# One row buffer for three edge passes of a two-layer graph network: gathers issued from the setup on, one a group in the first pass

## What is computed

```python
h = relu(layernorm(x))
# twice: xt = einsum('nd,rde->rne', h, W); msg = xt[rel, src]
#        h = relu(segment_sum(msg, dst) + h @ SW + b)
x = x + h
h = relu(layernorm(x))
edge_input = concat([h[src], h[dst], edge_attr])
msg = layernorm(relu(relu(edge_input @ eW1 + eb1) @ eW2 + eb2)) * eg + ebeta
node_agg = segment_sum(msg, dst)
upd = relu(concat([h, node_agg]) @ nW1 + nb1) @ nW2 + nb2
out = x + layernorm(h + upd) * ng + nbeta
```

## Time and profile before

| | us |
|---|---|
| median of 3 runs (lowest, highest) | 2863.91 (2858.38, 2866.82) |
| the profiled execution's own time | 2855.17 |
| its span, first to last instruction | 2853.5 |
| PE, DVE, ACT, POOL busy | 2187.5, 2023.0, 1541.0, 1821.7 |

### The profile page before, as it was taken

One profiled execution on the slowest core, in us unless ns is written; L12 is line 12 of the kernel. 1 busy time (PEld: TensorE's weight loads), 2 busy tenths in 40 slices (PEclk: granted clock), 3 DMA queues, 4 the chain that ended last, 5 costly groups with the idle time before them and its releaser, 6 DMA issues. The chain is left out here.

```text
span 2853.5 us, 54165 instructions
## 1 busy us (share of the span) xinstructions
PE 2187.5 (77%) x16219; PEld 1892.5 (66%) x16219; DVE 2023.0 (71%) x6854; ACT 1541.0 (54%) x3284; POOL 1821.7 (64%) x1381
## 2 busy tenths in 40 slices
PE   4778999999668899889873665577767766757997
PEld 4668988888668798888872565444444444435765
DVE  6887887878423587676755888676767676755999
ACT  5996656565423354444434877544334333425887
POOL 5763878765667188888866777288777777770000
PEclk9999999999889999999996888888888888888999
DMA  7994555545379644444437999666666666647998
GB/s 237 316 310 130 113 111 102 107 89 102 48 264 362 248 86 88 88 82 88 88 46 242 417 417 414 253 195 194 175 176 190 181 182 179 191 113 294 406 404 344
DMA packets 297971, 576.18 MB, mean 202 GB/s; under 512 B 65872, under 2 KB 147344, under 8 KB 297872
## 3 DMA queue, kind: packets, MB, share of 16 engines
q1 hardware_dynamic: 188112, 485.01, 46.9%
q0 software_dynamic: 109760, 90.00, 19.5%
HBM read 368.35 MB, written 206.50 MB: 201 GB/s over the span
## 5 line engine op out<-in xcount | busy, mean ns | idle before, releaser
L1056 POOL DMA_INDIRECT s<-E_summed,c_scat x392 | 652.1, 1664 | 262.6 <-ACT E_summed L1235 150.0
L1284 PE MATMUL ps<-c_w,E_masked 128*128 128x128 f32 x6272 | 722.6, 276 | 2.2 <-DVE E_masked L1087 2.0
L1284 PEld LDWEIGHTS ps<-c_w,E_masked 128*128 128x128 f32 x6272 | 714.1, 193 | 3.0 <-DVE E_masked L1087 3.0
L1087 DVE SCALAR_TENSOR_TENSOR E_masked<-E_type_row,E_hT 128x512 f32<-128x512 int32 x784 | 484.1, 688 | 74.4 <-ACT E_hT L1204 62.5
L365 POOL DMA_INDIRECT E_src_rows<-s,c_src x392 | 419.8, 1071 | 167.8 <-issue 118.0
L1418 POOL DMA_INDIRECT s<-E_summed,c_scat x196 | 335.8, 1713 | 126.3 <-issue 53.3
L1407 POOL DMA_INDIRECT E_ends<-h,c_near x196 | 220.1, 1123 | 91.0 <-issue 58.8
L1641 PE MATMUL ps<-E_same,E_normal 128*128 128x512 f32 (+3 forms) x392 | 175.1, 610 | 115.6 <-DVE E_normal L1501 115.6
L365 POOL DMA_INDIRECT E_src_rows<-in_x,c_src x196 | 191.6, 978 | 105.7 <-issue 74.3
L1235 ACT COPY E_summed<-ps 128x512 f32<-128x512 f32 x98 | 57.4, 586 | 347.1 <-DMA s<-E_summed,c_scat 347.0
L1641 PEld LDWEIGHTS ps<-E_same,E_normal 128*128 128x128 f32 x392 | 97.2, 259 | 222.5 <-DVE E_normal L1501 122.2
(11 more groups left out here) (134 smaller groups left out, 4378.8 us busy)
## 6 DMA issues: line engine op xcount, KB each, us to landing
s<-N_out SPq DMA_DIRECT2D x147, 512.0 KB, 5.3
N_xin<-in_x SPq DMA_DIRECT2D x98, 512.0 KB, 10.2
N_sin<-s SPq DMA_DIRECT2D x98, 512.0 KB, 6.8
E_dst_row<-in_dst_line SPq DMA_DIRECT2D x147, 256.0 KB, 4.5
E_type_row<-in_type SPq DMA_DIRECT2D x98, 256.0 KB, 3.5
N_xin<-s SPq DMA_DIRECT2D x49, 512.0 KB, 6.3
h<-N_h SPq DMA_DIRECT2D x49, 512.0 KB, 7.8
E_base<-s SPq DMA_DIRECT2D x49, 512.0 KB, 3.6
```

Of the source, the lines that this page charges most:

```text
L1056: pool.indirect_dma_start(s, bass.IndirectOffsetOnAxis(ap=c["scat"][:, k:k + 1], axis=0), summed[:, g % 2, t * D:(t + 1) * D], None, compu ...
L1087: nc.vector.scalar_tensor_tensor(out=masked[:, u % 2, r, :], in0=type_row[:, u, :], scalar=float(r), in1=hT[:, u % 2, :], op0=ALU.is_equal ...
L1284: ins = nc.tensor.matmul(ps[:, 2 + u % 2, t * D:(t + 1) * D], masked[:, u % 2, r, t * P:(t + 1) * P], w[:, r, :], start=(r == 0 and t == 0 ...
```

## The change

One buffer of 49 groups serves all three edge passes. It is allocated before the setup, and the setup issues the first 16 gathers (4 groups, `SETUP_AHEAD`) for E1 once the source indices are there; for this their load has a semaphore of its own, `src_loaded`. N0 goes on to group 40 instead of 36, and E1 then issues one gather a group instead of two. E2 is unchanged (28 groups ahead, two gathers a group). N2 issues all 49 groups for E3, and E3 issues no source gathers; the wrapped slots and the wait for `src_ready` are gone. `w1` and `w2` are released after E2, which makes room for the three groups.

```diff
-N0_AHEAD = 36
+SETUP_AHEAD = 4
+N0_AHEAD = 40
 N1_AHEAD = 28
-N2_AHEAD = 46
+N2_AHEAD = 49
...
-def setup(nc, sb, sem, a):
+def constants(sb):
...
+def setup(nc, sb, sem, c, ps, a, gathers):
...
-    first_loads = [(src[:], a["src"]), (dst[:], a["dst"])]
+    first_loads = [(c["dst"][:], a["dst"]), (c["sl1"][:], a["sl1"])]
...
+            sp.dma_start(src[:], a["src"]).then_inc(src_loaded, 16)
             for out, in_ in first_loads:
                 sp.dma_start(out, in_).then_inc(loaded, 16)
...
             pool.wait_ge(pool_done, 5)
-    return c
+            pool.wait_ge(src_loaded, 16)
+            gathers.issue(pool, a["x"], GT * SETUP_AHEAD)
...
 class Gathers:
-    def __init__(self, sb, sem, name, index, groups=GROUPS_E):
+    def __init__(self, rows, sem, name, index):
...
-                if g >= self.groups:
-                    pool.wait_ge(used, g - self.groups + 1)
...
             for g in range(GROUPS_E):
-                gathers.issue(pool, x, gathers.issued + 2)
+                gathers.issue(pool, x, gathers.issued + (1 if norm else 2))
                 scatter(g)
...
             for g in range(GROUPS_E):
-                sources.issue(pool, a["s2"], sources.issued + 1, src_ready)
                 for q in range(2):
...
+    with ExitStack() as edges:
+        gathered = edges.enter_context(nc.sbuf_tensor("gathered", [P, GROUPS_E * GE], F32))
+        first_rows, second_rows, sources = (
+            Gathers(gathered, sem, name, c["src"]) for name in ("E1_src", "E2_src", "E3_src"))
+        with ExitStack() as relational:
+            for name in ("w1", "w2"):
+                c[name] = relational.enter_context(nc.sbuf_tensor("c_" + name, [P, NREL, D], F32))
+            stage(setup, first_rows)
...
         stage(node_pass_2, sources)
         stage(edge_pass_messages, sources)
```

More of the change, by code:

```diff
@@ L207, in keep @@
         c[name] = sb("c_" + name, shape, dt)
[L208 to L218, removed]
+    for name in ("ident", "sl1", "nb2", "eb2", "sl2", "eW2", "nW2", "eW1s", "eW1d", "nW1x", "nW1m", "b2", "eg",
+                 "ebeta", "ng", "nbeta"):
+        keep(name, [P, D])
@@ new lines, in constants @@
+    keep("eW1e", [DE, D])
+    for name in ("b1", "eb1", "nb1", "eps", "one"):
+        keep(name, [P, 1])
+    keep("earlier", [P, WINDOW * P])
+    for name in ("nb2_parts", "eb2_parts"):
+        keep(name, [3 * QUARTER, 4, D], BF16)
+    keep("parts_weight", [3 * QUARTER, P], BF16)
+    for name in ("src", "dst", "near", "scat"):
+        keep(name, [P, TILES_E], I32)
+    for name in ("dstf", "dump_less_dst", "dump"):
+        keep(name, [P, TILES_E])
+    keep("zeros", [P, D])
+    return c
@@ L219, in setup @@
+def setup(nc, sb, sem, c, ps, a, gathers):
     part = sb("c_part", [P, D], BF16)
     rest = sb("c_rest", [P, D])
[L221 to L227, removed]
-    first_loads = [(src[:], a["src"]), (dst[:], a["dst"])]
[L230 to L233, removed]
+    first_loads = [(c["dst"][:], a["dst"]), (c["sl1"][:], a["sl1"])]
+    for name in ("nb2", "eb2"):
+        first_loads.append((c[name][:], a[name].partition_broadcast(P)))
@@ L243, in setup @@
-    loads.append((keep("nW1x", [P, D])[:], a["nW1"][0:D, :]))
-    loads.append((keep("nW1m", [P, D])[:], a["nW1"][D:2 * D, :]))
+        loads.append((c[name][:], a[name]))
+    loads.append((c["eW1s"][:], a["eW1"][0:D, :]))
+    loads.append((c["eW1d"][:], a["eW1"][D:2 * D, :]))
+    loads.append((c["eW1e"][:], a["eW1"][2 * D:2 * D + DE, :]))
+    loads.append((c["nW1x"][:], a["nW1"][0:D, :]))
+    loads.append((c["nW1m"][:], a["nW1"][D:2 * D, :]))
     for name in ("b2", "eg", "ebeta", "ng", "nbeta"):
-        loads.append((keep(name, [P, D])[:], a[name].partition_broadcast(P)))
+        loads.append((c[name][:], a[name].partition_broadcast(P)))
@@ L247, in setup @@
     for name in ("b1", "eb1", "nb1"):
-        loads.append((keep(name, [P, 1])[:], a[name].unsqueeze(1)))
+        loads.append((c[name][:], a[name].unsqueeze(1)))
+    src_loaded = sem("src_loaded")
+    ident, earlier, eps, one, parts_weight = (c[k] for k in ("ident", "earlier", "eps", "one", "parts_weight"))
+    src, dst, near, dstf, dump_less_dst, dump = (
+        c[k] for k in ("src", "dst", "near", "dstf", "dump_less_dst", "dump"))
+    bias_parts = [c["nb2_parts"], c["eb2_parts"]]
+    zeros = c["zeros"]
@@ L347, with issue @@
 class Gathers:
-    def __init__(self, sb, sem, name, index, groups=GROUPS_E):
+    def __init__(self, rows, sem, name, index):
         self.index = index
-        self.groups = groups
-        self.rows = sb(f"{name}_rows", [P, groups * GE])
+        self.rows = rows
         self.landed = [sem(f"{name}_landed{k}") for k in range(UNROLL)]
         self.issued = 0
-    def issue(self, pool, table, upto, used=None):
+    def issue(self, pool, table, upto):
         while self.issued < min(upto, TILES_E):
-            g, t = divmod(self.issued, GT)
-            if t == 0:
+            g = self.issued // GT
+            if self.issued % GT == 0:
                 wait(pool, self.landed[g % UNROLL], 64 * (g // UNROLL))
-                if g >= self.groups:
-                    pool.wait_ge(used, g - self.groups + 1)
-            at = (g % self.groups * GT + t) * D
             pool.indirect_dma_start(
-                self.rows[:, at:at + D], None, table,
+                self.rows[:, self.issued * D:(self.issued + 1) * D], None, table,
                 bass.IndirectOffsetOnAxis(ap=self.index[:, self.issued:self.issued + 1], axis=0)).then_inc(
@@ L1510, in step @@
                 if n:
-                    h = UNROLL * n[0] + n[1]
-                    wrapped = isinstance(h, int) and h >= sources.groups
-                    source_rows(*n, sources.group(h - sources.groups if wrapped else h))
+                    source_rows(*n, sources.group(UNROLL * n[0] + n[1]))
                     variances(*n)
@@ L1682, in graph_layers @@
     a["xsrc"] = nc.dram_tensor("xsrc", [GROUPS_E * P, GE], F32).ap()
-    c = setup(nc, sb, sem, a)
+    c = constants(sb)
     def stage(build, *args):
@@ L1689, in stage @@
             build(nc, own_sb, sem, c, ps, a, *args)
[L1691 to L1701, removed]
+    with ExitStack() as edges:
[6 more added lines that the diff above has]
+            stage(setup, first_rows)
+            stage(node_product, "N0", a["x"], a["s1"], c["sl1"], True, first_rows)
+            stage(edge_pass_relational, "E1", a["x"], a["s1"], c["w1"], True, first_rows)
+            stage(node_product, "N1", a["s1"], a["s2"], c["sl2"], False, second_rows)
+            stage(edge_pass_relational, "E2", a["s1"], a["s2"], c["w2"], False, second_rows)
         stage(node_pass_2, sources)
```

6 lines of the change are left out of this document (1 added, 5 removed).

## The result

The changed kernel takes **2754.86 us** (median of 4 runs, 2752.66 to 2755.85), the kernel before 2861.14 us in the same comparison (4 runs, 2823.34 to 2866.82): a ratio of 0.967, with an interval of 0.958 to 0.976. The forecast of no change, 2864 us (2848 to 2877), was wrong by 109 us.

What follows compares the result with a forecast made beforehand. Limits differ by block; in E1 and E3 the chain of scatters and their landing. Setup +6.4, E1 -1, N2 +3, E3 -8.3 sum to +0.1 us, 2855 us; shifted to the runs' median 2864 us, range 2848 to 2877.

Steps and rivals of the forecast that it cites:

- Setup: Before N0: 16 gathers delay the first load to 25.9 us; +6.4 us, bounds +3.7 and +10.6; N0 itself 0.
- the saved latency: N0's first load reaches DVE sooner, as the weights are in by then: 1.8 us back, between 0 and 2.7.
- the slower rival: End of setup: stretched gathers hold the barrier, first load at 34.9 us, kernel 11 us slower, 2875 us; chance 0.16.
- N1, E2, N2: N1 and E2 unchanged, 0, wrong if moved over 3 us; N2's twelve more gathers +3 us, bounds 0 and +4.9.
- E1: 36 groups with one gather instead of 26 with two, gathers all but free: -1 us, bounds -4 and 0.
- E3: Ten source gathers fewer on the path, 0.83 us each: -8.3 us, bounds -13 and 0.
- The faster rival: E1 and E3: gathers on POOL's queue are the path, saving 21 and 13 us; kernel -25 us, 2839; chance 0.17.
- the chain: E1: four scatters, their landing, four scatters set the pace, and two gathers fit into the landing; E3 the same with more.

Runs made afterwards that it cites:

- the burst run: Changed kernel, one gather a group in E1 but eight at once ahead of group 12's scatter: 2790.76 us, E1 562.1 us.
- SP's wait: SP's loads held until earlier scatters landed; added in E1 and E3 to the kernel before: 2786.44 us; in E1 to eight gathers at once: 2765.70 us.

## Why the prediction was wrong

**Setup: right.** First load at 26.24 us, forecast 25.9. The 2.4 us from POOL's end to the load came as taken from E3's end, and the saved latency was 2.5 us where I took 1.8. Setup and N0 together: +5.3 us, forecast +6.4. The sixteen gathers took 0.94 to 1.14 us beside DVE's copies, so the slower rival fell. The rule of the Trainium skill's page "SBUF — State Buffer", section "SBUF: two separate sides", by which they would have been stretched, shows no effect here; no row tells which of DVE's copies the rule covers.

**N1, E2, N2: right in size.** N2 +0.8 us (forecast +3). E2 moved by 2.1 us, N1 by 3.8; the latter is over the bound I set, but N1 varies by as much between profiles of the same code.

**E1: the step that failed**, and with it the forecast. I set 11.15 us a group with gathers beside 11.01 without and concluded that the gathers are all but free. Both figures are right; the comparison isn't. I took the 15 groups without gathers for what E1 costs when POOL has nothing else to do. But they came after the gathers in the same run and carried their lag; the burst run has the same 11.0 us after a single push. That the two figures are so close is chance: with two gathers POOL is full (11.06 us even where the loads are kept away from the landing), and without them it waits for a landing that the loads lengthen. The idle time ahead of each scatter, which I read as slack that hides a gather, was this landing, 3.56 us of gap in the mean where the changed kernel has 2.54. The trace held a hint that I cut off: my stretch ended at 714.33, and from 727.47 on the groups take 9.79 us. The forecast was -1 us with bounds of -4 and 0; measured are -50.4 us, by the profiles some 20 of lag and some 30 of POOL filled by two gathers.

**E3: the same step again.** I priced ten gathers at 15.85 - 15.02 = 0.83 us each, -8.3 us. With SP's wait, the kernel before still loses 9 us to the changed one (714.0 against 704.7), so that price was about right for what it measured. The other 52 us are, by that profile, the lag in the groups I had taken as the reference.

**The faster rival** had the direction and not the cause. It gave E1 21 us and E3 13, one gather's 1.32 us for each gather saved; measured are 112 us for 28 gathers, three times that. Its evidence against (11.15 beside 11.01) was the same false comparison. One row did speak: in the earlier trace rows no engine of E1 is busy for more than 86.5% of it. Groups of 11.0 us with no engine full need a reason; I named "the chain" and did not ask why its landing took up to 3.2 us, nor what else was under way meanwhile.

**Left open.** Whether the landing is late because packets of the two queues share the DMA engines or for another reason on the way to memory: the shares show only that they fall together. No run here frees ACT of its wait in groups without gathers, so what POOL's lag would cost if SP's loads did not follow it is known only from the runs with SP's wait. Open too is why runs of the same kernel lie 40 to 60 us apart where E3 can lag.

## What to carry to other kernels

Stretches of one run with and without a piece of work are not an experiment: what that work set off may last beyond it, so ask what state the reference stretch inherited. Where an engine lags with idle time of its own and no engine is full, look at when the other queue's transfers start within the period, level and lagging; a wait that seems to cost only freedom can put them where they cost less, as it did here. And in a loop with a landing in it, keep the work that fills the landing shorter than the landing: here one gather fits into 2.5 us, two with their issue (2.9 us) don't.

## What I had not expected of the hardware

The landing of four indirect scatters in E1, to the next group's first one, took 2.51 to 2.54 us in the mean where the DMA engines moved 41 to 48 GB/s in that time, and 3.64 us where they moved 142 GB/s; one gap of the kernel before has 155 GB/s and 4.01 us (611.33 to 615.34). The lag after one push of 8 us lasted for 28 groups, until SP had no loads left to send.
